# TensorE's signals in the three edge passes given by drains in place of the last matmul (graph kernel, one core)

## The reference

```python
# two mean-aggregating layers (SAGE)
agg  = segment_sum(x[src], dst, num_segments=n)
mean = agg / maximum(cnt, 1.0)[:, None]
h    = relu(mean @ W1_l.T + b1_l + x @ W1_r.T)      # layer 1; layer 2 the same on h, without relu
x    = layernorm(x + layer2)
# edge attention, 4 heads of 16
Qh, Kh, Vh = x @ Wq.T + bq, x @ Wk.T + bk, x @ Wv.T + bv
Ee    = edge_attr @ We.T + be
score = exp(clip((Kh[src] * Qh[dst] / sqrt(16) * Ee).sum(-1), -5, 5))
out   = layernorm(x + segment_sum(Vh[src] * score, dst))
```

## Time and profile before

| what | value |
|---|---|
| median of three runs | 12097.21 us |
| the profiled execution, its own time | 12102.03 us |
| its span | 12100.2 us |
| first pass, first to last gather | 10.4 to 3930.2 us |
| second pass | 4025.8 to 7929.7 us |
| third pass | 8134.6 to 12035.8 us |
| busy: POOL, PE, DVE, ACT | 8855.2, 7526.1, 3997.3, 1891.3 us |

### The profile page before, as it was taken

The page is one execution under the profiler, slowest core; times in us unless marked ns, Lnnn a source line. Parts: engine busy times, 40 slices in busy tenths (PEclk is TensorE's granted clock), DMA queues, the critical chain, the costliest instruction groups (busy, mean ns, idle before and its releaser), DMA issues.

```text
span 12100.2 us, 168544 instructions
## 1 busy us (share of the span) xinstructions
PE 7526.1 (62%) x44520; PEld 7023.2 (58%) x44521; DVE 3997.3 (33%) x8639; ACT 1891.3 (16%) x4110; POOL 8855.2 (73%) x9383
## 2 busy tenths in 40 slices
PE   4555556666666555555555555676666677777776
PEld 4555555555555544445555555565666666677776
DVE  2222222222222211111222222244455555555555
ACT  1000000000000100000000000022223333333333
POOL 6777777777777577777777777727777777777775
PEclk6555555555556555555555555555555555555555
DMA  3222222222222122222222222212322333333332
GB/s 69 60 59 54 60 60 60 58 60 59 59 59 55 45 48 48 48 47 48 46 47 48 48 47 48 47 42 79 80 79 78 80 79 80 79 79 80 78 80 72
DMA packets 915624, 741.93 MB, mean 61 GB/s; under 512 B 509830, under 2 KB 765478, under 8 KB 915479
## 3 DMA queue, kind: packets, MB, share of 16 engines
q0 software_dynamic: 300000, 410.20, 15.3%
q1 hardware_dynamic: 534004, 229.11, 7.9%
q10 hardware_dynamic: 81600, 102.41, 2.4%
HBM read 625.83 MB, written 115.24 MB: 61 GB/s over the span
## 4 chain that ended last, share of the span: by engine, by line
POOL 68%; issue 24%; PE 4%; DMA 1%; DVE 1%; POOLq 1%; DVEq 1%; ACT 0%; SPq 0%; ACTq 0%
POOL kv L436 68%; PE ps_kv L462 1%; PE ps_q L520 1%; DMA kv<-in_x,src_ids 1%; PE ps_sum L462 1%; POOLq L433 0%; PE ps_q L462 0%; DMA kv<-h_rows,src_ids 0%; DVE hot L836 0%; PE ps_t L514 0%; PE ps_kv L535 0%; DMA kv<-kv_rows,src_ids 0%; POOLq L221 0%; ACT stageT L639 0%; PE ps_t L528 0%
## 5 line engine op out<-in xcount | busy, mean ns | idle before, releaser
L436 POOL DMA_INDIRECT kv<-kv_rows,src_ids x3125 | 2950.4, 944 | 1155.7 <-issue 948.4
L436 POOL DMA_INDIRECT kv<-h_rows,src_ids x3125 | 2953.1, 945 | 1046.4 <-issue 1038.5
L436 POOL DMA_INDIRECT kv<-in_x,src_ids x3125 | 2950.6, 944 | 978.7 <-issue 937.7
L462 PE MATMUL ps_q<-kv,hot 128*128 128x65 f32 x5000 | 1126.7, 406 | 1246.2 <-DMA kv<-h_rows,src_ids 650.0
L462 PEld LDWEIGHTS ps_q<-kv,hot 128*128 128x128 f32 x5000 | 1063.2, 317 | 1382.0 <-issue 1382.0
L836 DVE SCALAR_TENSOR_TENSOR hot<-dst_ids,base,ps_t 128x640 f32<-128x640 f32 (+2 forms) x1629 | 1434.1, 880 | 1028.5 <-issue 958.1
L462 PE MATMUL ps_sum<-kv,hot 128*128 128x65 f32 x5000 | 1068.5, 390 | 1115.0 <-DMA kv<-in_x,src_ids 478.2
L462 PEld LDWEIGHTS ps_sum<-kv,hot 128*128 128x128 f32 x5000 | 999.8, 300 | 1229.0 <-issue 1228.8
L462 PE MATMUL ps_kv<-kv,message 128*128 128x65 f32 x4440 | 1038.2, 417 | 970.4 <-DMA kv<-h_rows,src_ids 378.2
L462 PEld LDWEIGHTS ps_kv<-kv,message 128*128 128x128 f32 x4440 | 973.3, 327 | 1042.6 <-issue 1041.3
L565 PE MATMUL ps_sum<-message,node_h 128*128 128x64 f32 x6260 | 1466.4, 421 | 0.2 <-DVE message L984 0.2
(11 more groups left out here) (166 smaller groups left out, 6897.9 us busy)
## 6 DMA issues: line engine op xcount, KB each, us to landing
node_q<-in_edge_attr SPq DMA_DIRECT2D x125, 480.0 KB
edge_space<-ee_rows SPq DMA_DIRECT2D x125, 480.0 KB
kv<-in_x,src_ids POOLq DMA_INDIRECT x3125, 2.4
kv<-h_rows,src_ids POOLq DMA_INDIRECT x3125, 2.4
kv<-kv_rows,src_ids POOLq DMA_INDIRECT x3125
node_q<-in_edge_attr SPq DMA_DIRECT2D x125, 320.0 KB
edge_space<-ee_rows SPq DMA_DIRECT2D x125, 320.0 KB
ee_rows<-node_q ACTq DMA_DIRECT2D x25, 1440.0 KB, 5.7
```

Source lines behind the costliest of these rows:

```text
L436: nc.gpsimd.indirect_dma_start(out=into[:, u, k, 0:width], out_offset=None, in_=table_rows, in_offset=bass.IndirectOffsetOnAxis(ap=src_ids ...
L462: mm = nc.tensor.matmul(to[:, 0:D + 1], one_hots[:, k, :], kv[:, u, k, 0:D + 1], start=(k == 0), stop=(k == K - 1))
```

## The change

Six places are touched: `sum_group`, `turn_attr`, `edge_products`, `turn_hots`, `sum_messages` and the end of `extra_queries`. In each the increment moves from the last matmul or transpose to a drain behind it (`nc.tensor.drain(fusable=False)`), an instruction of PE's own queue that is done when what was issued ahead of it is done. The signals of the extra turns (`x.hot_t`, L577), of the extra queries (`x.query`, L579), of the setup and of the dense stages stay on the matmuls.

```diff
--- before.py
+++ after.py
@@ -457,28 +457,32 @@
             last.then_inc(wT, 1)
             pe.wait_ge(w_ready, 1)
 
+            def through():
+
+                return nc.tensor.drain(fusable=False)
+
             def sum_group(to, one_hots, u, done):
                 for k in range(K):
-                    mm = nc.tensor.matmul(to[:, 0:D + 1], one_hots[:, k, :], kv[:, u, k, 0:D + 1],
-                                          start=(k == 0), stop=(k == K - 1))
-                mm.then_inc(done, 1)
+                    nc.tensor.matmul(to[:, 0:D + 1], one_hots[:, k, :], kv[:, u, k, 0:D + 1],
+                                     start=(k == 0), stop=(k == K - 1))
+                through().then_inc(done, 1)
 
             def turn_attr(i, e, landed):
                 pe.wait_ge(attr_in, landed)
 
                 pe.wait_ge(ee_copied, e + 1)
                 for pair in range(PAIRS):
-                    tp = nc.tensor.transpose(ps_t[:, pair * P:(pair + 1) * P], attr[:, i, pair * P:(pair + 1) * P], ident[:])
-                tp.then_inc(ee_turned, 1)
+                    nc.tensor.transpose(ps_t[:, pair * P:(pair + 1) * P], attr[:, i, pair * P:(pair + 1) * P], ident[:])
+                through().then_inc(ee_turned, 1)
 
             def edge_products(e):
 
                 pe.wait_ge(ee_copied, e + 2)
                 nc.tensor.matmul(ps_e[:, 0:PAIRS * P], ones16[:], be_parts[:].rearrange("p i d -> p (i d)"), start=True, stop=False)
                 for pair in range(PAIRS):
-                    mm = nc.tensor.matmul(ps_e[:, pair * P:(pair + 1) * P], attrT[:, pair, :], we2[:],
-                                          start=False, stop=(pair == PAIRS - 1))
-                mm.then_inc(ee_made, 1)
+                    nc.tensor.matmul(ps_e[:, pair * P:(pair + 1) * P], attrT[:, pair, :], we2[:],
+                                     start=False, stop=(pair == PAIRS - 1))
+                through().then_inc(ee_made, 1)
 
             def sum_pairs(p, phase, first_e, per):
                 assert per < SLOTS
@@ -541,8 +545,8 @@
                 pe.wait_ge(p.hot, g + 1)
                 hold(pe)
                 for k in range(K):
-                    tp = nc.tensor.transpose(ps_hot[:, k * P:(k + 1) * P], hot[:, u, k, :], ident16[:])
-                tp.then_inc(p.hot_t, 1)
+                    nc.tensor.transpose(ps_hot[:, k * P:(k + 1) * P], hot[:, u, k, :], ident16[:])
+                through().then_inc(p.hot_t, 1)
 
             def query_rows(to, turned, block_rows):
 
@@ -562,8 +566,8 @@
 
             def sum_messages(to, one_hots, messages, done):
                 for k in range(K):
-                    mm = nc.tensor.matmul(to, one_hots[:, k, :], messages[:, k, :], start=(k == 0), stop=(k == K - 1))
-                mm.then_inc(done, 1)
+                    nc.tensor.matmul(to, one_hots[:, k, :], messages[:, k, :], start=(k == 0), stop=(k == K - 1))
+                through().then_inc(done, 1)
 
             def extra_queries(p, x, word, u):
                 before, first, more = word
@@ -578,7 +582,8 @@
                         pe.wait_ge(x.hot_c, n + 1)
                         query_rows(ps_query[u], hotT_x, q_block_x).then_inc(x.query, 1)
 
-                nc.tensor.matmul(ps_query[u][:, 0:1], ones16[:], zeros16[:, 0:1], start=False, stop=True).then_inc(p.query, 1)
+                nc.tensor.matmul(ps_query[u][:, 0:1], ones16[:], zeros16[:, 0:1], start=False, stop=True)
+                through().then_inc(p.query, 1)
 
             def extra_sums(x, word, u):
                 before, first, more = word
```

## The result

The kernel after takes 12411.25 us (median of three runs, 12410.8 to 12411.7) against 12097.21 us: 314 us more, ratio 1.026, 95% interval 1.0245 to 1.0274. I had forecast 12100 us, 3 us more, and a range up to 12121 us.

The account below looks back on a forecast made before the run. POOL's gathers were taken to bound the kernel, with most drains hidden. Signal lateness 0.2, backlog 1.5 and the third end 1.2 us made 2.9 us on the 12097.2 us median, forecast 12100 us, range 12095 to 12121 us.

Parts of the forecast that it names:

- What bounds the kernel: Whole kernel: POOL's gathers set the pace, 1.249 us each in the third pass; messages ready 15.6 us ahead.
- the count: All passes: 4669 drains added, 1444 and 1250 in the sum passes and 1975 in the third; no matmul removed.
- Price of one drain: Each drain on PE: 0.34 us from the lost overlap with the next weight load, range 0 to 0.53 us.
- The price of 0.19 us: Each drain on PE, by the skill's row-group rule: no weight-load overlap to lose, only a single-column matmul's depth, 0.19 us.
- The clean period: Third-pass groups where PE never waits: PE's period 4.8 in place of 3.76 us; over 5.4 us would show the forecast wrong.
- The other marks: Signs of error: POOL waiting over 0.3 us on messages or one-hots, third pass over 3901 us; L975's wait forecast near 10 us.
- Third pass, steady part: Last 62 groups: 132 drains, 45 us, fit in 52.6 us of L975's waits; groups with extras absorb theirs; backlog 1.5 us.
- Sum passes: End of first pass, 430 us: drains of 59 us, 92 at most, hidden in PE's 117 us of waits for gathers.
- Ends of the passes: After each pass's last gather nothing hides drains: 0.1 us at each of the first two ends, 1.2 us at the third.
- PE becomes the bound at the end of the third pass: Rival: in the last two 62-group stretches, 408 drains exceed 122 us in hand; 12125 us, chance 0.11 (over 12121 us).
- the 12191 us of every drain on the chain: Rival's upper figure, end of third pass: all 408 drains at 0.53 us, 216 us against 122 in hand, 94 us over.
- It costs nothing: Rival, all drains on PE: the drain retires with the last matmul, price near 0; 12097 us, chance 0.27.

Follow-up runs that it names:

- query_only: Against the kernel before with masked table words: of all drains only the 626 behind the queries' single column; 12115.78 us, ratio 1.0016.
- bare_drains: Masked kernel after with signals back on the last matmuls and a drain that signals nothing behind each; 12396.84 us, ratio 1.0249 to the kernel before.
- before_masked: Kernel before with the first field of each table word masked to 17 bits, one more register operation, same result; 12097.17 us, ratio 1.0000.
- drains_twice: Masked kernel after with two drains at each place, the second signalling; 17211.5 and 17218.0 us where the kernel before takes 15.87 ms, ratios 1.0854 and 1.0852.
- sum_only_2: Repeat run with only the 723 drains behind the sums of messages; this kernel's two runs 16104.3 and 16107.4 us, ratios 1.0152 and 1.0151 to the kernel before.

## Why the prediction was wrong, step by step

**What bounds the kernel** held: POOL's pitch is still 1.249 us where PE lets it, 802 gathers in the pass's first 1000 us. So did the count: the trace has 4669 drains.

**"Price of one drain": mis-sized, 0.34 us forecast, 0.49 us measured** (0.53 with the term left out above), at the upper end of my bounds. The part that I saw, the lost overlap and a restart, is 0.42 to 0.45 us: 0.20 us of overlap between the matmuls and 0.22 of standstill, where I had 0.30 between matmul and load and 0.04. The price of 0.19 us, by which no overlap was there to lose, isn't borne out. The part that I did not see is the sequencer's own work, 0.2 us behind the query of a plain group and the load of the words at the head of a turn. I had looked for rows of PE and PEld only, and never at what PE's sequencer does between two groups, though the kernel reads a table there. The clean period came out at 5.25 us (4.8 forecast), under the 5.4 that I had named as the mark of a wrong price: that mark was set too far out. The other marks spoke: POOL waited up to 4.2 us for the message, where 0.3 was the limit, the third pass took 4153 us and not 3901, and VectorE's wait for gathers in its last 387 us went to nothing, not to 10 us.

**"Third pass, steady part": this is the step that failed.** I let the groups with an extra swallow a third of the drains and then set the other two thirds against the 52.6 us that L975 waited for gathers. This is cover counted twice. The waits of PE at extras and the waits of VectorE for gathers belong to one slack: a core that is later at an extra reaches the next gather later. Both shrink together in query_only (106.1 to 46.9 us and 119.1 to 37.3) and are nearly or wholly gone in the kernel after. The rows give for all of it 0.68 us a group, 42 us in 62 groups. Against that stand 204 drains x 0.49 = 100 us. Even with my own price, 204 x 0.34 = 69 us, the cover would have been short by 27 us, more than the 15.6 us of POOL's slack. query_only shows the exchange, 61.7 us of new idle time against 59.2 us of old.

**"Sum passes": forecast hidden, measured 38.3 us with both ends.** I had set 59 us of drains, 92 at most, against 117 us of waits for gathers, and put the clock at "a few more matmuls at the low level" without a number. The 117 us were all used up: PE is idle 77 us more for other things and busy 37.7 us more, at a matmul of 420 ns throughout. So the drains' term was mis-sized and the clock's was put at nothing. At the end of the pass the rest of the core is so late that POOL is held: it waits 3.89 us for a one-hot at 3942.72, right behind a head of a turn.

**"Ends of the passes"**: +1.2 us forecast for the third, +25.1 measured; +0.1 forecast for the first, +15.4 measured. I had put the backlog at 1.5 us because POOL "isn't held". But as soon as the core is slower than POOL, the backlog grows until POOL is held, and it all lies in the tail. The last message comes 30.9 us after the last gather's start where it came 6.8 us after it: +24.1, of which 17 are the slack, which is 17.9 us at the last pair before and 0.8 after, and the other 7 are about what five groups' drains cost at 1.49 us each. Behind the last message it is +1.2 us, the amount that I had forecast for the end alone, though with a price that was too small. In the first pass the last sum ends 20.6 us after the last gather's start in place of 5.2, which is the whole +15.4.

**The rival.** "PE becomes the bound at the end of the third pass" was the right mechanism, and its chance of 0.11 and its price of 12125 us were too small; the 12191 us of every drain on the chain were too. It asked at which price the last 124 groups would run over, and all that I had counted for it was those. With the cover at 0.68 us a group in place of 0.85 and a third of the drains besides, PE is slower than POOL in a much longer part: POOL's gathers in 1000 us are 802, 789, 734 and 694 from 8200, 9200, 10200 and 11200 us on. "It costs nothing" is refuted by the result, and by bare_drains even without the late signals. These are worth 27.8 us in all; what one of them is worth no run shows.

What I can't close: for 11200 to 12000 us the terms match the period, but I have not split the 0.72 us ahead of the transposes between restart, register work and load; the load was partly exposed before. That the mask's one operation a word costs 13.4 us behind the drains, and nothing without, shows the register work's part only in kind. How much of the sum passes' 38.3 us is the clock's is open too.

## What to carry to other kernels

A drain on TensorE in place of a signal on the last matmul cost about half a microsecond here where PE sets the pace, and what it costs depends on what the sequencer has to do next: put loads of registers, loops and branches ahead of it, under running matmuls. Before calling such a cost hidden, add up the engine's own waits per unit of work once, and don't count the waits of the engine that it feeds a second time. If a pace is kept by a buffer's slack, then once the balance tips the whole slack shows up at the end besides. And before a run with one instruction more is read as its price, look whether the trace has the instruction.

## What the runs showed of the hardware that was not expected

- TensorE's sequencer works far ahead of the array: a load of seven words lasting 1.70 us runs under ten matmuls of 2.4 us and leaves 0.34 us. With a drain between, the same place takes 2.85 us.
- 4669 drains that signal nothing cost 299.7 us (bare_drains against before_masked). A second drain behind a first lasts 13 ns and starts 62 ns behind it (drains_twice).
- With drains in the sum passes the fp32 matmuls of the sums last 420 ns throughout, the time of the 1.2 GHz level, where the mean before was 390, 406 and 417 by buffer. At the end of the first pass PE is busy 307.6 us of 430 in place of 270.0 and yet on the lower level.
- On some chips the kernel before takes 15.87 ms, and a sum's result is taken up 18.2 us after the modelled end; drains there last up to 29.6 us (sum_only_2), where the longest elsewhere is 2.40 us (bare_drains). On the other chips each drain of the kernel after ends 0.02 to 0.05 us behind the modelled end of the matmuls: a drain's row tells by how much that model is off.
